# One kernel, three re-ordered stages: local attention, small-head softmax attention and split experts

## The reference, cut to what matters

```
x = x + 0.5 * experts(layernorm(x))         # top-1 of 8 experts, hidden 512, a * sigmoid(g)
x = x + softmax_attention(layernorm(x))     # 16 heads of 8 channels, rotary, causal, T = 256
x = x + 0.5 * experts(layernorm(x))         # the same weights again
x = x + 0.5 * local_block(layernorm(x))     # depth 2: local attention + gated ffn
x = x + retention(layernorm(x))             # 16 heads, decay mask, no softmax
x = x + 0.5 * local_block(layernorm(x))     # the same weights again
```

```
qkv = shift_token(x) @ wqkv                 # 8 heads of 64 channels
q, k = l2norm(q) * qs, l2norm(k) * ksc      # then rotary with a position scale
sim = q @ k^T, window of 64 tokens back     # keys at a distance of 0 to 64
out = softmax(sim) @ v;  x = x + out @ wo
```

## Time and profile before

| what | us |
|---|---|
| median of 3 runs (3563.79 to 3576.41) | 3569.26 |
| profiled execution | 3566.36 |
| its span in the trace | 3564.6 |
| softmax attention, from the trace | 544.6 |
| local attention, four stages, each | 400.2 |
| experts, two stages | 141.6 and 139.2 |
| retention | 302 |

### The profile page before, as it was taken

The page is one execution under the profiler, slowest core; times in us unless marked ns, Lnnn a source line. Parts: engine busy times, 40 slices in busy tenths (PEclk is TensorE's granted clock), DMA queues, the critical chain, the costliest instruction groups (busy, mean ns, idle before and its releaser), DMA issues. The chain is left out here.

```text
span 3564.6 us, 61785 instructions
## 1 busy us (share of the span) xinstructions
PE 2947.5 (83%) x19174; PEld 1858.4 (52%) x19174; DVE 1953.8 (55%) x4255; ACT 1635.5 (46%) x4692; POOL 1620.3 (45%) x1763
## 2 busy tenths in 40 slices
PE   4384888888567699998899988777799998899988
PEld 2382555555366356553565643555356563465653
DVE  2261454545245377763577743656477774577754
ACT  2142333333233466663566653111466664466653
POOL 0433000000233588881788850000088883488870
PEclk8696898999689799999999999878899999999999
DMA  4111000000011100000000000000000000000000
GB/s 174 41 37 28 1 1 0 0 0 1 15 39 37 52 1 0 0 0 0 1 0 0 0 0 0 1 0 0 1 1 0 0 0 1 1 1 0 0 0 24
DMA packets 27960, 40.69 MB, mean 11 GB/s; under 512 B 4688, under 2 KB 24656, under 8 KB 27088
## 3 DMA queue, kind: packets, MB, share of 16 engines
q1 hardware_dynamic: 12528, 25.89, 1.9%
q0 software_dynamic: 4096, 8.40, 0.8%
q10 hardware_dynamic: 11232, 5.12, 0.5%
HBM read 25.42 MB, written 13.96 MB: 11 GB/s over the span
## 5 line engine op out<-in xcount | busy, mean ns | idle before, releaser
L260 ACT ACTIVATE la_pr<-psum,la_nm 128x128 f32<-128x128 f32 (+1 forms) x1024 | 389.0, 392 | 498.8 <-DVE la_nm L292 496.8
L286 DVE TENSOR_TENSOR la_t<-psum,tabs 128x512 f32<-128x512 f32 x256 | 177.1, 692 | 469.7 <-ACT la_sq L246 459.7
L225 POOL TENSOR_TENSOR la_t<-la_t,la_tS 128x512 f32<-128x512 f32 x256 | 402.4, 1572 | 23.9 <-POOL la_tS L221 7.6
L221 POOL TENSOR_TENSOR la_tS<-la_t,tabs 128x512 f32<-128x512 f32 x256 | 326.5, 1275 | 160.6 <-DVE la_t L287 160.5
L217 POOL TENSOR_SCALAR la_pr<-la_pr,la_rl 128x192 f32<-128x192 f32 x512 | 384.3, 762 | 0.1
L828 POOL TENSOR_TENSOR sa_qk<-z 128x512 f32<-128x512 f32 x32 | 40.5, 1266 | 701.3 <-DVE z L914 458.2
L297 DVE SCALAR_TENSOR_TENSOR la_qk<-la_rn,la_t 128x512 f32<-128x512 f32 x256 | 320.1, 1250 | 0.0
L130 PE MATMUL psum<-la_hT,big 128*128 128x256 f32 x1024 | 294.9, 411 | 23.0 <-POOL la_hT L205 18.2
L170 PE MATMUL psum<-la_sq,cf 128*128 128x512 f32 x512 | 292.9, 654 | 9.6 <-ACT la_sq L246 9.6
L180 PEld LDWEIGHTS psum<-cf,la_pr 128*128 128x128 f32 x1536 | 177.0, 141 | 181.4 <-POOL la_pr L217 98.3
L180 PE MATMUL psum<-cf,la_pr 128*128 128x128 f32 x1536 | 214.7, 276 | 27.6 <-POOL la_pr L217 26.8
(11 more groups left out here) (169 smaller groups left out, 6259.0 us busy)
## 6 DMA issues: line engine op xcount, KB each, us to landing
big<-early SPq DMA_DIRECT2D x1, 6688.0 KB, 32.1
ex_xb<-sorted_x SPq DMA_DIRECT2D x78, 64.0 KB, 1.8
sorted_y<-ex_out ACTq DMA_DIRECT2D x78, 64.0 KB, 1.6
big<-late SPq DMA_DIRECT2D x1, 3114.0 KB, 10.3
cf<-const SPq DMA_DIRECT2D x1, 2265.5 KB, 13.0
x<-x_t SPq DMA_DIRECT2D x1, 2048.0 KB, 8.0
sorted_x<-z SPq DMA_DIRECT2D x1, 2048.0 KB, 34.4
x_final<-x SPq DMA_DIRECT2D x1, 2048.0 KB, 7.2
```

What stands on the lines that cost most here:

```text
L221: pool.tensor_tensor(tS[:, :], t2[:, :], tab[:, 1, :], ALU.mult).then_inc(ts_ready, 1)
L225: pool.tensor_tensor(t3[:, j % 2, :], t1[:, :], tS[:, :], ALU.add).then_inc(summed, 1)
L260: ins = act.activation(pr[:, j % 2, h, c0:c1], s_ps[h][:, s0:s0 + c1 - c0], ACT.Exp, bias=nm[:, j % 2, t, h:h + 1], accum_out=ls[:, j % 2, ...
```

## The change

Three stages are touched; retention keeps the old function. In `local_attention` the order inside a step changes on all four engines (the maxima, exponentials, scaling, transposes and output keep their units and steps except as noted), the exponentials of a unit run one step later on ACT, Ln and Exp too, and the two POOL multiplies of the second half become one `tensor_tensor` with a broadcast scale. Softmax attention gets a function of its own, `small_head_softmax`: scores once, with queries on partitions; a maximum, an exponential with its sum and a scaling before a transpose by PE, as local attention has them; scores doubly buffered, probabilities in four slots; the rotation by a shuffle instead of two more projections. In `experts` PE takes a before down, and DVE takes the output one step later and first.

```diff
@@ local_attention, tensor @@
                 for s, b, k, j in steps(i):
+                    u = s - 1
+                    if runs(u, U):
+                        pe.wait_ge(sq_ready, u + 1)
...
+                        mm(ss_ps[:, :], g.head64[:, :], sq[:, :], start=True, stop=True).then_inc(ss_ready, 1)
...
-                    if runs(s, U):
-                        pe.wait_ge(sq_ready, s + 1)
...
-                        mm(ss_ps[:, :], g.head64[:, :], sq[:, :], start=True, stop=True).then_inc(ss_ready, 1)
@@ local_attention, gpsimd @@
-                        for h in range(2):
-                            x = pr[:, (j - 3) % 2, h, P + PAD:3 * P]
-                            ins = pool.tensor_scalar(x, x, rl[:, (j - 3) % 2, 1, h:h + 1], None, ALU.mult)
-                        ins.then_inc(normed, 1)
+                        x = pr[:, (j - 3) % 2, :, P + PAD:3 * P]
+                        pool.tensor_tensor(x, x, rl[:, (j - 3) % 2, 1, :].unsqueeze(2).to_broadcast([P, 2, 2 * P - PAD]), ALU.mult).then_inc(normed, 1)
+                    if j == 1 and runs(b + 1, B):
+                        carry(b + 1, 1 - k)
...
-                    if j == 1 and runs(b + 1, B):
-                        carry(b + 1, 1 - k)
@@ local_attention, scalar: new order exp(s-3), Ln/Exp(s-1), sq(s), v(s-1), pt(s-3) @@
+                    u = s - 3
+                    if runs(u, U):
+                        act.wait_ge(nm_ready, u + 1)
...
+                        ins.then_inc(p_ready, 1)
+                    u = s - 1
+                    if runs(u, U):
+                        act.wait_ge(ss_ready, u + 1)
...
+                        act.activation(rn[:, :], lnn[:, :], ACT.Exp, scale=-0.5, bias=g.tiny[:, 1:2]).then_inc(rn_ready, 1)
@@ local_attention, vector: new order 1/ls(s-3), qk(s-1), t1/t2(s), maxima(s-2), residual, pt(s-3), oT(s-4) @@
+                    u = s - 3
+                    if runs(u, U):
+                        dve.wait_ge(p_ready, u + 1)
...
+                    u = s - 1
+                    if runs(u, U):
+                        dve.wait_ge(rn_ready, u + 1)
+                        dve.wait_ge(summed, u + 1)
+                        if at_least(u, 2):
+                            dve.wait_ge(s_ready, u - 1)
+                        dve.scalar_tensor_tensor(qk[:, (j - 1) % 2, :], rn[:, :], 1e12, t3[:, (j - 1) % 2, :], ALU.min, ALU.mult).then_inc(qk_ready, 1)
@@ new: small_head_softmax, tensor @@
+                    if runs(s, U):
+                        jj, bank = e // 2, s_ps[e % 2]
+                        if e % 2 == 0:
+                            pe.wait_ge(rows_done, 4 * b + jj + 1)
+                        if at_least(s, 2):
+                            pe.wait_ge(p_ready, s - 1)
+                        for n in range(2):
+                            mm(bank[n].rearrange("p (a n) -> p a n", a=4)[:, 0:4:2, :], g.ident[:, :], g.tri_q.unsqueeze(1).to_broadcast([P, 2, P]),
+                               start=True, stop=False, skip_group_check=True)
+                        for t, cols in ((0, slice(0, P)), (1, slice(P, TRI))):
+                            for n in range(2):
+                                q = 2 * (e % 2) + n
+                                head = qks[32 * q:32 * q + 32, k, jj, :]
+                                ins = mm(bank[n][:, cols], head[:, t * P:(t + 1) * P], head[:, T:T + (t + 1) * P], start=False, stop=(t == 1), skip_group_check=True)
+                        ins.then_inc(s_ready, 1)
+
+                    if runs(b + 1, B):
+                        if e == 0:
+                            project(b + 1)
+                        if e in (3, 4):
+                            spread(b + 1, e - 3)
+                        if e == 5:
+                            values(b + 1)
+                        if e in (6, 7):
+                            spread(b + 1, e - 4)
...   transposes of unit s-3 (six a step), products with v of unit s-5 in odd steps
@@ new: small_head_softmax, gpsimd @@
+                        pool.wait_ge(rl_ready, u + 1)
+                        for t, (c0, c1) in enumerate(((0, P), (P, TRI))):
+                            x = pr[:, ee % SLOTS, :, c0:c1]
+                            ins = pool.tensor_tensor(x, x, rl[:, ee % 2, t, :].unsqueeze(2).to_broadcast([P, 2, c1 - c0]), ALU.mult)
+                        ins.then_inc(normed, 1)
+                    if e == 1 and runs(b + 1, B):
+                        total(b + 1)
+                    if e == 3 and runs(b + 1, B):
+                        carry(b + 1)
@@ new: small_head_softmax, scalar @@
+                        for t, (c0, c1) in enumerate(((0, P), (P, TRI))):
+                            for h in range(2):
+                                ins = act.activation(pr[:, ee % SLOTS, h, c0:c1], s_ps[ee % 2][h][:, c0:c1], ACT.Exp,
+                                                     bias=nm[:, ee % 2, t, h:h + 1], accum_out=ls[:, ee % 2, t, h:h + 1])
+                        ins.then_inc(p_ready, 1)
...   then biased (e 0), high (e 2), values (e 5), output (e 4), and the copy of one half of pt of unit s-3
@@ new: small_head_softmax, vector @@
+                dve.tensor_tensor(t1, xb[:, :], tab[:, 0, :], ALU.mult)
+                dve.stream_shuffle(turn[:, :], xb[:, :], [lane ^ 1 for lane in range(32)]).then_inc(swapped, 1)
+                dve.wait_ge(swapped, b + 1)
+                dve.tensor_tensor(t2, turn[:, :], tab[:, 1, :], ALU.mult).then_inc(turned, 1)
...
+                        dve.tensor_reduce(nm[:, e % 2, 0, :], s_pair[e % 2][:, :, 0:P], AX.X, ALU.max, negate=True)
+                        dve.tensor_reduce(nm[:, e % 2, 1, :], s_pair[e % 2][:, :, P:TRI], AX.X, ALU.max, negate=True).then_inc(nm_ready, 1)
...   then 1/ls of unit s-1, rotate (e 1), low (e 2), rows_out (e 3, 4, 6, 7), the other half of pt of unit s-3
@@ experts, tensor @@
+                        if at_least(u, 2):
+                            pe.wait_ge(y_ready, u - 1)
+                        up(a_ps[m], m, 0).then_inc(a_ready, 1)
                     u, m = s - 2, k
...
-                    u, m = s - 1, 1 - k
-                    if runs(u, BLOCKS):
-                        if at_least(u, 2):
-                            pe.wait_ge(y_ready, u - 1)
-                        up(a_ps[m], m, 0).then_inc(a_ready, 1)
@@ experts, vector: new order out(s-3), weight copy(s-1), y(s-1); the store on ACT is of s-4 @@
```

309 lines of the change are left out of this document (265 added, 44 removed).

## The result

The changed kernel took 3427.05 us (median of 4 runs, 3421.82 to 3438.15), the kernel before 3568.31 beside it: ratio 0.9606, interval 0.9575 to 0.9637. The forecast was 3379, the range 3290 to 3480. The sign and the range held; the gain is 141 us where 190 was said.

A forecast was written before the change was run, and what follows sets the result against it. Local attention was taken as bound by one ring through ACT and DVE, experts by PE waiting for y. 3566.4 + 25 (local attention) - 169 (softmax attention) - 46 (experts) = 3376 profiled, 3379 as median; range 3290 to 3480.

The forecast's parts named there:

- bound of -52: Experts: the larger-gain end of the forecast -46 us, whose other bound was -18 (3.2 us a step).
- The two rings: Local attention: one wait cycle through ACT and DVE, one over POOL and DVE, both 6.1 us a step.
- POOL's gain of 0.56 us is thus needed: Local attention: POOL's cheaper second multiply pays for the new place of `qk`; without it the step would be 6.7 us.
- The bump: Softmax attention: steps e = 1 to 3 take about 10 us instead of 6.4, behind the next block's preparation.
- the 2.2 us of the loads: Softmax attention: ACT's load per step, with DVE and POOL nearly level; a floor of 17.6 us a block.
- the price of the clock: Softmax attention: PE's time at 1.2 GHz costs 0 to 60 us, taken as 15.
- a share under 0.8: Softmax attention: a granted PE clock below this would show the forecast wrong; 0.85 was assumed.
- A: Softmax attention: preparation delays passed between engines, or PE's low clock, cost six us more a block; +95, 3475; chance 0.18.
- B: Local attention: `carry` and POOL's order against `qk` give 6.4 us a step; +75, 3455; chance 0.12.
- C: Local attention: port free for `qk`, 5.8 us a step; softmax attention nears its floor; 3275; chance 0.14.
- D: Local attention: PE drops to 1.2 GHz; with half the steps low +420, 3800; chance 0.03.
- E: Old order still decides: local attention stays at 400, experts at 139, only softmax attention gains; 3400; no separate chance.

The follow-up runs named there:

- la_two_scalars: Changed kernel with POOL's second multiply in local attention taken back to two tensor_scalar instead of one tensor_tensor; 3422.32 us in one run.
- best_v1: Changed kernel with the softmax attention of mix_a and the local attention of la_two_scalars, experts left as changed; 3363.74 us, ratio 0.9432.
- sm_fill: Changed kernel with the two mask matmuls of each softmax attention step issued three times, scores unchanged; 3438.59 us in one run.
- sm_both_first: Changed kernel, softmax attention: PE's transposes before the preparation's matmuls, DVE's copy of the transposes before the preparation's work; 3391.26 us, ratio 0.9493.
- mix_b: Changed kernel: mix_a's softmax with preparation respread; local attention in the old order with one tensor multiply; experts with PE's old order; 3424.83 us, ratio 0.9629.
- mix_a: Changed kernel: sm_both_first plus small-head product before transposes; local attention with early scores, two scalar multiplies; experts with DVE's old order; 3482.69 us, ratio 0.9794.

## Why the prediction was right, and where it was not

**Experts: right.** Forecast a step of 2.85 and -46 us; measured 2.77 and 2.79 a step in the two stages and -52.4 in all, just beyond the bound of -52. PE is idle before L1517 4.5 us in both stages together. The weight copy takes 1.09 in the middle, not the 1.35 of the earlier trace rows. That row was no usual one: in the kernel before, the median of this copy is 0.49, so the new order, in which it stands beside POOL's copy, has made it longer. The cells above add what the forecast only assumed: DVE's new order is needed, and is worth a quarter to a third of the gain.

**Local attention: the size near, by luck in part; one reason wrong.** Forecast +25, measured +15.5. The two rings are there and level, at 5.98 in place of 6.1: `qk` cost 0.86 from start to start (forecast 1.15), because POOL's multiply took 0.83, not the estimated 0.94, and ends sooner; L222 and L226 both take 1.27, without the 1.51 of the earlier trace rows; and with `carry` the average step is 6.06, not 5.98. What was wrong is "POOL's gain of 0.56 us is thus needed". The forecast took `qk`'s delay as the same behind any POOL instruction; la_two_scalars shows it only behind the two-input form. So the change from scalar to tensor form made the wait that it was thought to pay for: with the new order and the old form the four stages take 1600.9 us against 1600.8 before (1597.3 in best_v1). In the new order the whole +15.5 thus comes with the form, not with the new place of `qk`.

**Softmax attention: the mechanism partly, the size not.** Forecast -169, measured -101.7. The bump nearly held: 11.4 us for "about 10", with its order of events (rotation, total, high, low) as written. Two steps failed.

The first is the sentence behind the bump, "The later spreads and values wait for copies that are done a step before", with the five other steps at the 2.2 us of the loads: they took 3.1 each. The working followed ACT and DVE and never PE's queue, in which the transposes stand behind spreads that wait for the low part. By blocks: 5.6 us over 21.2, sixteen times, make 90 us; 15 of them were in the sum as the price of the clock, and fill and drain took 14 (442.9 less 16 times 26.8), not 22. 90 - 15 - 8 = 67, the whole of what is missing in this stage.

The second is the price of the clock, 15 us for the stage. In the changed kernel gap 3 took 3.07 us at full clock and 5.06 at the low one (2 and 7 samples), gap 4 2.27 and 3.58 (6 and 5), with the same order on every engine; gap 5, at full clock in 8 of its 13 blocks, took 2.6 there and 2.99 on average. Taking the full-clock values for the averages gives 1.2, 0.5 and 0.4 us a block, and gap 2 gives 1.1 by the block of sm_fill: some 3.2 us a block, 50 a stage. This is an estimate, and its gap 2 rests on one sample. By it, over half of the missing 67 us is the mis-sized clock, and the rest the waits in the queues at full clock.

**The clock.** The text called a share under 0.8 a sign of being wrong; it was 0.79. The price can't be taken apart from the order: the low stretches come behind PE's standstills, and cost most where the transposes stand late in PE's step. sm_both_first still has the low clock in gap 2 and takes 2.27 there; its clock is 0.89 and the stage 42 us shorter. No run holds the clock at full with the order of the changed kernel and no added work, so the exact shares stay open.

**The rivals.** A, six us more a block, names what happened: 5.6 more, by delays handed from engine to engine and by PE's low clock, which makes transposes and spreads late. Its total of 3475 was too high since it added them to a sum that already had the clock's 15 us and a long fill, and since experts and local attention came out 16 us better. B (6.4 a step) did not come: 6.06. C asked for `qk` at 0.67 and 5.8 a step; the changed kernel has 0.94. la_two_scalars has 0.69, and its steps are 5.73 to 5.94 but for the one behind `carry`, 6.27, so that 0.06 a step is gained over before and not 0.2. The Trainium skill, "SBUF — State Buffer", section "Who interferes with whom", has the engine that issues first keep the shared pair for its whole instruction. The `tensor_tensor` rows agree but for 0.15 us (`qk`, 0.69 us when alone, is done 0.54 behind L217's end). The `tensor_scalar` rows do not: POOL had issued first, and yet `qk` took 0.70 us or less in 224 of 256 cases; the running multiply was left alone or, where `qk` came within 0.06 us of its start, took up to 1298 ns where 757 is its shortest. Nothing of D: 0.98 to 1.00 in local attention. E is contradicted by experts at 114.

## What to carry to other kernels

In a pipeline written by hand, sum up a step along each engine's queue, PE's included, and over two steps as well as one: here the costly waits stood between queues (a copy behind a rotation on DVE, transposes behind spreads on PE), and each of the two repairs alone lost 7 us where both gained 42. Put what the next unit's exponential needs first in every queue, and try asking for a piece of the preparation a whole step later behind its source: gaps 1 and 2 together took 6.1 us in mix_b, which does that, and 7.3 in sm_both_first, though no run changes this alone. Read the steps of a stage at either level of the clock apart: an average share of 0.79 hid steps of 3.07 and 5.06 us. An edit that pays off alone, or doesn't, says little of what it does beside another: read every stage for itself and check the pair.

## What the runs showed of the hardware that was not expected

- POOL's `tensor_scalar` and `tensor_tensor` with a broadcast scale treat DVE differently: `qk` took a median of 692 ns beside the first and 939 beside the second, and the first, or the next one behind it, was stretched in return (above).
- The multiply with a broadcast scale is cheaper for its size than the one with two full inputs: 512 elements in 1048 ns and 384 in 827, against 1267 for L795 and L222. The groups of the softmax stage:

```profile
L806 POOL TENSOR_TENSOR ss_pr<-ss_pr,ss_rl 128x512 f32<-128x512 f32 x128 | 134.1, 1048 | 0.0
...
L795 POOL TENSOR_TENSOR ss_qk<-z 128x512 f32<-128x512 f32 x16 | 20.3, 1267 | 12.8 <-DVE z L892 12.8
```

- Retention, the same code in all kernels, took 301.6 to 302.3 us at a granted clock of 0.81 in most, 305.8 at 0.79 in mix_a, 308.1 to 308.3 at 0.78 in four, and 312.7 at 0.77 in la_two_scalars:

```profile
2061.00:2374.00 313.00, 236.81 (x1984) 164.41 (x1984) 182.02 (x368) 40.89 (x96) 28.77 (x34) 0.77 0.00 0
```

  With the earlier trace rows that is 10 us more PE time for the same 1984 matmuls. The code doesn't differ, so a stage left alone can move a comparison of this kernel by 0.3%. Each kernel was profiled once, so whether the length belongs to the kernel or changes from one execution to the next isn't known, nor what sets it.
